# Turning the softmax maxima on VectorE, squares on GpSimd, and a new order of the starts, in a two-block transformer kernel

## The chip, the cores and the metric

The kernel runs as one program on one core of one Trainium2 chip (trn2). The metric is the device time of one execution in microseconds. A core has five engines with queues of their own: TensorE (PE), VectorE (DVE), ScalarE (ACT), GpSimd (POOL) and SyncE (SP), which here only issues DMAs. They wait for each other on semaphores.

## The reference

Two transformer blocks on x [B=8, T=512, C=256], float32. Each block is modulated by a vector made from c, with layer norm ahead of each half:

```python
h = _layernorm(x) * (1 + ca) + sa
x = x + ga * _L0_attn_ref(h, ...)      # rms-normed q and k, rope, 16 heads of 16, softmax(q k / 4 + 1)
h = _layernorm(x) * (1 + cb) + sb
x = x + gb * _L0_ffn_ref(h, ...)       # ternary weights, 1024 wide
# the second block the same way:
x = x + ga * _L1_attn_ref(h, ...)      # biases, no rms norm, no rope; output divided by its mean norm
x = x + gb * _L1_ffn_ref(h, ...)       # layer norm, 8 experts of 1024, gelu, next_w
```

The change touches the two attention halves only. In layer 0 they are

```python
q = (x @ wq.T).reshape(B, T, H, hd); k = ...; v = ...
q, k = rms(q), rms(k)                  # var = mean(t * t, axis=-1) + EPS over the 16 of a head
q, k = rope(q), rope(k)
scores = einsum('bhtd,bhsd->bhts', q, k) * scale + 1.0
y = einsum('bhts,bhsd->bhtd', softmax(scores), v) @ wproj.T
```

## The kernel before

The program runs four parts one after the other: attention of layer 0 (to about 583 us), the feed-forward net of layer 0 (to about 1282 us), attention of layer 1 (1282 to about 1812 us) and the experts (to the end). The change lies in `attention(nc, layer, d, keep)`, which builds the first and third.

Precision: float32 products are made of fp16 high and low halves. Queries and keys stand in SBUF as `QS` and `KT`, 128 partitions x 8 head pairs x 512 tokens, in two blocks of partitions (a = 0 and 1, one head of each pair). A block holds three runs of 16 rows, high and low halves, so that one matmul over 48 rows gives the score. A 49th row of `QS` (index QROWS - 1) carries the negated maximum of each query, and a matmul over 49 rows gives the score less its maximum.

Order of the work: a table gives every step of a batch its slot. `PAIRS` = 32 slots are one batch, 8 slots are one group G of four heads, and each engine runs `for p in range(BEGIN, END)` through the same slots in order. `AT0` and `AT1` hold the slots of the steady state, relative to their batch; `EARLY0` and `EARLY1` those of the first batches, from slot -140 on, ahead of slot 0 of batch 0. In slot p TensorE does: raw scores 2p+AHEAD (L1028, into one of two banks `SM`), the two final scores of pair p (L1045, into `ST`), raw scores 2p+AHEAD+1, then the slot's job, and the products with the values (L1064, into `AV`). `raw` waits until VectorE has read the bank two raws before.

- The maximum. VectorE reduces each 128x512 block of raw scores (L824) to one column of `M`, negated, fp16. In slot 8G-5 the job `MT` has TensorE turn `M` by four transposes (L964) into the PSUM bank `X`; ScalarE copies it to `MTs` (L596, 4 x 512) a slot later; and SyncE copies it a slot after that by two DMAs (L356) of two partitions each into the 49th rows. The first scores of the group (slot 8G) wait for these. `M` and `MTs` are doubled.
- The bank `X`. It is shared by all jobs outside the start: T0, T1 (turning the normed tokens, L969), QK0 to QK3 and V0, V1 (projections, L934), H0 to H3 (turning q and k, L1000), YT, P and MT. They go through it in the order of `jobs`, and each waits until the one before was copied out (`out`).
- Layer 0 norm and rope. After each QKi ScalarE reads the bank twice: Copy to `qraw` (L613) and Square to `sq` (L616). VectorE sums the squares by head (L886, step SUM), GpSimd adds epsilon (VAR, L533), ScalarE makes the first guess of the root (RMSG, L706 and L708), GpSimd does a Newton step (INV, L455 to L461) and the rotation (ROT, L488 to L502, about 5.1 us a tile), ScalarE the high half (HI, L718), GpSimd the low half (LOW, L510).
- To the heads' layout. The H jobs turn q and k, VectorE copies them out (L841), SyncE stores four tiles of 256 KB a batch to DRAM (`store_features`, L332, tensor `qk`) and loads them as 12 DMAs of 128 KB (HIGH and LOWS, L343 and L349), 16 partitions each. In layer 1 ScalarE and GpSimd make the halves from the projections directly.
- Weights for the next part. In layer 0, 32 parts of the feed-forward weights are loaded, split by GpSimd (L449, L451), checked by VectorE with one maximum each (L891) and stored, at the slots of `STAGE_AT`: four a batch.
- Modulation. Three groups of small matmuls, at the slots of `MOD_AT`.
- The tokens of batch n+1 are loaded (L361, `xt`) after XN of batch n has read those of batch n; STAT (L868) reads them.

The scores of a group's first slot wait for its two row copies:

```python
if u == 0 and a == 1:
    pe.wait_ge(row_ld[G % 2], 32 * (G // 2 + 1))
```

Of the kernel before, what the change touches and what calls it, by code (L numbers as in the profile page):

```python
# [109 lines left out]
AHEAD = 28  # L110


def placed(base, table):
# [27 lines left out]
OWN_BANK = {("T0", 0): "X", ("T1", 0): "AV", ("V0", 0): "SM0", ("V1", 0): "SM1"} | {(f"QK{i}", 0): f"ST{i}" for i in range(4)}
OWN_BANK0 = OWN_BANK | {(f"QK{i}", 1): f"ST{i}" for i in range(4)} | {(f"H{i}", 0): ("X", "AV", "SM0", "SM1")[i] for i in range(4)}
STAGE_AT = [PAIRS * (i // 4) + (20, 22, 25, 27)[i % 4] for i in range(4 * B)]


def attention(nc, layer, d, keep):
# [28 lines left out]
    with ExitStack() as ctx:  # L175
# [393 lines left out]
        def _(act):  # L569
# [73 lines left out]
            for p in range(BEGIN, END):  # L643
# [1442 lines left out]
```

## Time and profile before

| | |
|---|---|
| time, 3 runs | 2191.36, 2195.03, 2197.32 us; median 2195.03 us |
| profiled execution | 2191.5 us, its span 2189.8 us |
| TensorE matmuls | 1880.9 us busy (86%), x10573 |
| weight loads | 767.0 us (35%) |
| VectorE | 1350.6 us (62%), x2591 |
| ScalarE | 1211.6 us (55%), x1686 |
| GpSimd | 576.3 us (26%), x668 |
| DMA | 147.90 MB, mean 68 GB/s, q1 25.3% of 16 engines |

The span runs from the first to the last instruction of the profiled execution; the execution's own time is 1.7 us longer. The busy shares are means over four parts with different limits, so the two attention parts are read by windows of time. The batches of layer 0 lie at 109.5 to 172.5, 172.5 to 235.4, 235.4 to 296.9, 296.9 to 358.2, 358.2 to 419.2, 419.2 to 481.7, 481.7 to 536.8 and 536.8 to 583.2 us. Those of layer 1 begin at 1357.0, 1416.0 and 1478.3 us; the last ends at 1812.3 us. The times ahead of 109.5, and from 1282.0 to 1357.0, are the starts of the two layers.

### The profile page before, as it was taken

To read this page: it belongs to the slowest core of one execution; us is meant where nothing else is said; L and a number is where in the kernel's file an instruction comes from. 1 tells how busy PE (TensorE), PEld (TensorE's weight loads), DVE (VectorE), ACT (ScalarE), POOL (GpSimd) and SP (SyncE) were. 2 spreads that over 40 slices of the span, in tenths; PEclk is the share of its full clock that TensorE was granted. 3 is DMA by queue.
4 is the path that set the end of the run, shared out by engine and by line. 5 is a ranking of instruction groups with operands and counts; after the bars stand their busy time and mean duration, and the time that the engine had idled before them with its cause. 6 is when DMAs were issued, how large, how long until landed. Compare 5 with 4: busy or idle time off the path is not lost. (4 is left out here: it accounts for less than half of the span.)

```text
span 2189.8 us, 29709 instructions
## 1 busy us (share of the span) xinstructions
PE 1880.9 (86%) x10573; PEld 767.0 (35%) x10573; DVE 1350.6 (62%) x2591; ACT 1211.6 (55%) x1686; POOL 576.3 (26%) x668
## 2 busy tenths in 40 slices
PE   5789999988759999999999956898889983888897
PEld 3323333222224444444444421232223221444443
DVE  5578888878433553553554424777777873677672
ACT  4377888767623432432432233787778873565563
POOL 4676766642200000000000041111111001343443
PEclk8689999999969999999999975999999996899999
DMA  2343554433260000000000023333333304323210
GB/s 107 69 112 88 122 131 108 121 109 85 73 232 1 20 21 12 10 20 11 10 20 1 10 67 53 59 59 59 69 68 59 59 11 160 116 92 129 89 39 19
DMA packets 111985, 147.90 MB, mean 68 GB/s; under 512 B 11874, under 2 KB 95188, under 8 KB 109780
## 3 DMA queue, kind: packets, MB, share of 16 engines
q1 hardware_dynamic: 111828, 145.77, 25.3%
q8 instruction: 103, 1.69, 0.3%
q14 instruction: 54, 0.44, 0.1%
HBM read 100.34 MB, written 45.14 MB: 66 GB/s over the span
## 5 line engine op out<-in xcount | busy, mean ns | idle before, releaser
L824 DVE TENSOR_REDUCE A_M<-A_SM 128x1 f16<-128x512 f32 x1024 | 652.8, 685 | 179.2 <-PE A_SM L1028 177.1
L587 ACT ACTIVATE A_P<-A_ST 128x1024 f32<-128x1024 f32 x512 | 524.0, 1026 | 152.8 <-PE A_ST L1045 148.2
L1028 PE MATMUL A_SM<-A_KT,A_QS 48*128 48x512 f16 x1024 | 358.3, 404 | 78.4 <-DVE A_M L824 67.8
L1337 PE MATMUL B_PA<-B_Hh,B_wh 128*128 128x512 f16 x1024 | 388.1, 379 | 0.0
L1337 PE MATMUL B_PA<-B_Hl,B_wh 128*128 128x512 f16 x1024 | 388.1, 379 | 0.0
L1241 ACT ACTIVATE B_af<-B_PA,B_sv 128x512 f32<-128x512 f32 x192 | 132.0, 688 | 358.1 <-PE B_PA L1337 358.0
L1045 PE MATMUL A_ST<-A_QS,A_KT 49*128 49x512 f16 x1024 | 304.9, 391 | 0.1
L1064 PE MATMUL A_AV<-A_P,A_V 128*32 128x512 f32 x2048 | 280.0, 610 | 5.6 <-ACT A_P L587 5.0
L1028 PEld LDWEIGHTS A_SM<-A_KT,A_QS 48*128 48x128 f16 x1024 | 81.7, 94 | 461.0 <-DVE A_M L824 403.6
L1302 DVE TENSOR_SCALAR B_Hh<-B_af 128x512 f16<-128x512 f32 x128 | 57.9, 452 | 269.7 <-ACT B_af L1241 269.7
L1197 POOL TENSOR_TENSOR B_hl<-B_hf,B_hh 128x512 f16<-128x512 f32 x16 | 18.5, 1157 | 547.8 <-ACT B_hh L1224 547.8
L1337 PEld LDWEIGHTS B_PA<-B_Hl,B_wh 128*128 128x128 f16 x1024 | 100.2, 98 | 119.3
L1337 PEld LDWEIGHTS B_PA<-B_Hh,B_wh 128*128 128x128 f16 x1024 | 100.2, 98 | 119.2
L1304 DVE SCALAR_TENSOR_TENSOR B_Hl<-B_af,B_Hh 128x512 f16<-128x512 f32 x128 | 88.7, 693 | 4.4
L559 POOL TENSOR_TENSOR A_tr<-A_qkf,A_tr 128x512 f16<-128x512 f32 x32 | 37.0, 1159 | 196.5 <-ACT A_tr L681 196.4
L1296 DVE SCALAR_TENSOR_TENSOR B_uf<-B_PD,B_sv,B_af 128x512 f32<-128x512 f32 x64 | 47.8, 747 | 48.4 <-PE B_PD L1337 24.3
L520 POOL TENSOR_TENSOR A_hl<-A_hf,A_hh 128x512 f16<-128x512 f32 x32 | 36.8, 1158 | 121.0 <-ACT A_hh L665 121.0
L1064 PEld LDWEIGHTS A_AV<-A_P,A_V 128*32 128x32 f32 x2048 | 44.6, 108 | 63.7 <-issue 50.3
L868 DVE BATCH_NORM_STATS2 A_st<-A_xt 128x6 f32<-128x256 f32 x64 | 25.1, 416 | 65.6 <-DMA A_xt<-x_tok 60.0
L1337 PE MATMUL B_PA<-B_hh,B_wh 128*128 128x512 f16 x128 | 51.1, 399 | 14.3 <-issue 14.3
L1045 PEld LDWEIGHTS A_ST<-A_QS,A_KT 49*128 49x128 f16 x1024 | 55.8, 94 | 15.3 <-ACT A_P L587 12.6
L969 PE MATMUL A_X<-id,A_xn 128*128 128x128 f32 x120 | 22.8, 321 | 44.5 <-ACT A_xn L688 29.0
(308 smaller groups left out, 3335.8 us busy)
## 6 DMA issues: line engine op xcount, KB each, us to landing
D_w_st<-in_we_dram SPq DMA_DIRECT2D x16, 1024.0 KB, 4.9
qk<-A_tr SPq DMA_DIRECT2D x62, 256.0 KB, 2.4
A_KT<-qk SPq DMA_DIRECT2D x96, 128.0 KB, 4.7
A_QS<-qk SPq DMA_DIRECT2D x96, 128.0 KB, 5.2
A_w_st<-in_w_ffn_dram SPq DMA_DIRECT2D x32, 352.0 KB, 3.8
w_hi<-A_f_hi SPq DMA_DIRECT2D x32, 176.0 KB, 3.5
w_lo<-A_f_lo SPq DMA_DIRECT2D x32, 176.0 KB, 3.6
B_wl<-w_lo SPq DMA_DIRECT2D x1, 5632.0 KB, 25.1
```

The costliest lines, as they stand in the source:

```text
L520: nc.gpsimd.tensor_tensor(hl[:, f, :], hf[:, f, :], hh[:, f, :], ALU.subtract).then_inc(h_low, 1)
L559: nc.gpsimd.tensor_tensor(tr[2 * (i // 2) + 1][:, i % 2, :], qkf[:, i % 2, :], tr[2 * (i // 2)][:, i % 2, :], ALU.subtract).then_inc(qk_lo ...
L587: nc.scalar.activation(P[:, st, 2 * pair:2 * pair + 2, :], ST[:, u % 2, :, :], ACT.Exp, scale=1.0 / math.sqrt(HD)).then_inc(exp_s, 1)
L824: nc.vector.tensor_reduce(M[G % 2][:, tt, o:o + 1], SM[:, n % 2, :], AX, ALU.max, negate=True).then_inc(max_s, 1)
L1028: nc.tensor.matmul(SM[:, n % 2, :], QS[b % 2][r, 2 * g + pair, tt * 128:tt * 128 + 128], KT[b % 2][r, 2 * g + pair, :], start=True, stop=T ...
L1045: ins = nc.tensor.matmul(ST[:, u % 2, a, :], KT[b % 2][r, pair, o:o + 128], QS[b % 2][r, pair, :], start=True, stop=True)
L1064: ins = nc.tensor.matmul(AV[32 * j:32 * j + 32, :], V[b % 3][:, st, g * HG + j, :], P[:, st, j, :], start=st == 0, stop=st == TT - 1)
L1241: nc.scalar.activation(af[:, s % 3, :], PA[:, s % 4, :], ACT.Silu if s < HM else ACT.Gelu, scale=sv[:, which, m:m + 1]).then_inc(a_out, 1)
L1296: nc.vector.scalar_tensor_tensor(out=uf[:, s % 2, :], in0=PD[:, s % 2, :], scalar=sv[:, 1, s:s + 1], in1=src, op0=ALU.mult, op1=ALU.mult). ...
L1302: nc.vector.tensor_scalar(Hh[w][:, m, :], src, HS, None, ALU.mult).then_inc(high, 1)
L1304: nc.vector.scalar_tensor_tensor(out=Hl[w][:, m, :], in0=src, scalar=HS, in1=Hh[w][:, m, :], op0=ALU.mult, op1=ALU.subtract).then_inc(spli ...
L1337: ins = nc.tensor.matmul(out, a, c, start=start and kt == 0 and n_ == 0, stop=stop and kt == kts[-1] and n_ == len(ops) - 1)
```

## The change

1. The job MT is gone. VectorE writes the maxima into `M` [128, 32] and, in slot 8G-5 after its first maximum, transposes the 32x32 blocks of `M` into `rows`. SyncE copies these a slot later (8G-4) with eight DMAs of 8 partitions x 64 bytes each. `X16` and `MTs` are gone. GpSimd clears `M` once.
2. `AHEAD` is 26 for 28.
3. In layer 0, from batch 2, ScalarE reads a QK bank once (Copy) and GpSimd squares `qraw` into `sq`, in the slots SQ. SUM, VAR, RMSG, INV, ROT, HI and LOW come one to three slots later.
4. Both starts have new tables. In layer 0: earlier transposes and projections of batch 1, HI and LOW of batch 0 between them, H jobs two slots earlier, tokens of later batches normed at other slots, the third part of the modulation earlier. In layer 1: all QK projections of batch 1 ahead of the loads, in banks of their own, and GpSimd's clearing of the second buffers after batch 1's low halves.
5. The weight parts: two a batch in batches 0 to 4, and 22 every third slot from 185 to 248.
6. The DRAM tensor `qk` is laid out by head block, so that a load reads 8 KB in one run per partition, and a store writes with the head index within four as its outermost dimension.

```diff
 PAIRS = 32
-AHEAD = 28
+AHEAD = 26
...
 AT0 = placed(-80, dict(STAT=(-51, -48, -45, -43), AGG=-41, ROOT=-40, XN=(-27, -26, -24, -22), T0=-1, T1=1, HH=(0, 2), HL=(1, 3),
-                       QK0=10, QK1=12, QK2=18, QK3=20, V0=26, V1=28, SUM=(12, 14, 20, 22), VAR=(15, 24), RMSG=(16, 26),
-                       INV=(17, 27), ROT=(17, 21, 27, 31), HI=(22, 27, 35, 37), LOW=(24, 28, 36, 38),
+                       QK0=10, QK1=12, QK2=18, QK3=20, V0=26, V1=28, SQ=(11, 13, 20, 22), SUM=(14, 15, 23, 24), VAR=(16, 26), RMSG=(17, 27),
+                       INV=(18, 28), ROT=(18, 22, 29, 32), HI=(23, 28, 36, 38), LOW=(25, 29, 37, 39),
...
                             QK0=10, QK1=11, QK2=12, QK3=13, V0=14, V1=15, SUM=(12, 13, 15, 15), VAR=(13, 15), RMSG=(13, 15),
-                            INV=(14, 17), ROT=(16, 16, 17, 17), HI=(17, 18, 19, 20), LOW=(18, 19, 20, 21),
-                            H0=30, H1=31, H2=32, H3=33, HIGH=(36, 36, 36, 36, 37, 37, 37, 37), LOWS=(38, 38, 38, 38))),
-          placed(-140, dict(STAT=(10, 10, 10, 10), AGG=11, ROOT=11, XN=(16, 16, 16, 16), T0=21, T1=23, HH=(22, 24), HL=(23, 25),
-                            QK0=25, QK1=26, QK2=27, QK3=28, V0=40, V1=42, SUM=(29, 29, 34, 35), VAR=(30, 34), RMSG=(31, 35),
-                            INV=(32, 37), ROT=(33, 36, 48, 50), HI=(37, 39, 128, 133), LOW=(38, 40, 129, 134),
+                            INV=(14, 17), ROT=(16, 16, 17, 17), HI=(17, 19, 22, 24), LOW=(18, 20, 23, 25),
+                            H0=28, H1=29, H2=30, H3=31, HIGH=(34, 34, 34, 34, 34, 34, 34, 34), LOWS=(35, 35, 35, 35))),
+          placed(-140, dict(STAT=(10, 10, 10, 10), AGG=11, ROOT=11, XN=(16, 16, 16, 16), T0=18, T1=20, HH=(19, 21), HL=(20, 22),
+                            QK0=23, QK1=24, QK2=25, QK3=26, V0=32, V1=33, SUM=(27, 27, 33, 33), VAR=(28, 34), RMSG=(29, 40),
+                            INV=(30, 42), ROT=(31, 41, 44, 45), HI=(39, 42, 129, 133), LOW=(40, 43, 130, 134),
                             H0=137, H1=139, H2=140, H3=141, HIGH=(143, 143, 144, 144, 145, 145, 146, 146), LOWS=(147, 147, 148, 148))),
-          placed(-140, dict(STAT=(35, 35, 36, 36), AGG=37, ROOT=37, XN=(41, 41, 41, 41), T0=44, T1=46, HH=(45, 47), HL=(46, 47))),
-          placed(-140, dict(STAT=(127, 128, 130, 131), AGG=132, ROOT=133, XN=(135, 136, 138, 139))),
-          dict(STAT=(4, 5, 6, 6))]
+          placed(-140, dict(STAT=(18, 18, 18, 18), AGG=19, ROOT=26, XN=(31, 31, 31, 31), T0=35, T1=37, HH=(36, 38), HL=(37, 39))),
+          placed(-140, dict(STAT=(128, 129, 130, 131), AGG=132, ROOT=135, XN=(143, 144, 146, 147))),
+          dict(STAT=(10, 11, 12, 13), AGG=(14,), ROOT=(15,))]
 EARLY1 = [placed(-140, dict(STAT=(0, 0, 0, 0), AGG=1, ROOT=2, XN=(3, 3, 3, 3), T0=4, T1=5, HH=(5, 6), HL=(6, 7),
-                            QK0=10, QK1=11, QK2=12, QK3=13, V0=14, V1=15, HIGH=(18, 18, 18, 18, 19, 19, 19, 19), LOWS=(20, 20, 20, 20)))]
-MOD_AT = (-138, -134, -106)
+                            QK0=10, QK1=11, QK2=12, QK3=13, V0=14, V1=15, HIGH=(18, 18, 18, 18, 18, 18, 18, 18), LOWS=(19, 19, 19, 19))),
+          placed(-140, dict(STAT=(12, 12, 12, 12), AGG=13, ROOT=13, XN=(21, 21, 21, 21), T0=23, T1=25, HH=(24, 26), HL=(25, 27),
+                            QK0=28, QK1=29, QK2=30, QK3=31, HIGH=(36, 36, 36, 36, 36, 36, 36, 36), LOWS=(38, 38, 38, 38))),
+          placed(-140, dict(STAT=(132, 133, 135, 136), AGG=137, ROOT=138, XN=(142, 144, 146, 150))),
+          dict(STAT=(13, 14, 16, 17), AGG=(18,), ROOT=(19,))]
+MOD_AT = (-138, -134, -120)
+MOD_PE = (-138, -134, -118)
 OWN_BANK = {("T0", 0): "X", ("T1", 0): "AV", ("V0", 0): "SM0", ("V1", 0): "SM1"} | {(f"QK{i}", 0): f"ST{i}" for i in range(4)}
-OWN_BANK0 = OWN_BANK | {(f"QK{i}", 1): f"ST{i}" for i in range(4)} | {(f"H{i}", 0): ("X", "AV", "SM0", "SM1")[i] for i in range(4)}
-STAGE_AT = [PAIRS * (i // 4) + (20, 22, 25, 27)[i % 4] for i in range(4 * B)]
+OWN_BANK |= {(f"QK{i}", 1): f"ST{i}" for i in range(4)}
+OWN_BANK0 = OWN_BANK | {(f"H{i}", 0): ("X", "AV", "SM0", "SM1")[i] for i in range(4)}
+STAGE_AT = [PAIRS * b + o for b in range(B - 3) for o in (21, 25)] + [PAIRS * B - 71 + 3 * i for i in range(22)]
...
         QS = [sb(f"QS{k}", [128, H // 2, T], F16) for k in range(2)]
-        M = [sb(f"M{k}", [128, TT, HG], F16) for k in range(2)]
-        MTs = [sb(f"MT{k}", [HG, T], F16) for k in range(2)]
+        M, rows = ([sb(f"{n}{k}", [128, 32], F16) for k in range(2)] for n in ("M", "rows"))
...
-            return d["qk"][n % 2, which, :, :].rearrange("(p a d) t -> a d p t", a=2, d=HD)[a]
+            return d["qk"][n % 2, which, a, :, :, :]
...
                     sp.wait_ge(qk_ld[n % 2], 192 * (n // 2))
-                sp.dma_start(d["qk"][n % 2, which, :, :].rearrange("(f p) t -> p f t", p=128), tile[:, :, :]
+                sp.dma_start(d["qk"][n % 2, which, :, :, :, :].rearrange("a d (f q) t -> q (a d) f t", f=FT), tile[:, :, :]
...
             for p in range(BEGIN, END):
-                G = group_at(p, -3)
+                G = group_at(p, -4)
                 if G is not None:
-                    sp.wait_ge(*out("MT", G))
+                    sp.wait_ge(row_s, G + 1)
+                    g, k = G % NG, (G // NG) % 2
                     for a in range(2):
-                        sp.dma_start(QS[(G // NG) % 2][BLK * a + QROWS - 1:BLK * a + QROWS, 2 * (G % NG):2 * (G % NG) + 2, :],
-                                     MTs[G % 2][2 * a:2 * a + 2, :]).then_inc(row_ld[G % 2], 16)
+                        row = QS[k][BLK * a + QROWS - 1:BLK * a + QROWS, 2 * g:2 * g + 2, :].rearrange("o p (t x) -> o (p t) x", t=TT)
+                        for i in range(4):
+                            sp.dma_start(row[:, :, 32 * i:32 * i + 32], rows[G % 2][32 * i + 8 * a:32 * i + 8 * a + 8, :]
+                                         ).then_inc(row_ld[G % 2], 16)
...
                 un = qraw[:, tt, :]
-                pool.wait_ge(q_raw, r + 1)
+                if n == 1:
+                    pool.wait_ge(q_raw, r + 1)
...
                         nc.gpsimd.tensor_tensor(hl[:, f, :], hf[:, f, :], hh[:, f, :], ALU.subtract).then_inc(h_low, 1)
-                if p == slots_of("HL", 0)[1] + 1:
+                if p == slots_of(*(("HL", 0) if L0 else ("HL", 1)))[1] + 1:
                 if L0:
+                    for tt in range(TT):
+                        n = at(p, "SQ", tt)
+                        if n is not None and n >= 2:
+                            pool.wait_ge(*out(f"QK{tt}", n))
+                            pool.wait_ge(q_sum, TT * n + tt - 1)
+                            nc.gpsimd.tensor_tensor(sq[:, tt % 2, :], qraw[:, tt, :], qraw[:, tt, :], ALU.mult).then_inc(q_sq, 1)
...
-                if name == "MT":
-                    act.wait_ge(*done(name, n))
-                    if n >= 2:
-                        act.wait_ge(row_ld[n % 2], 32 * (n // 2))
-                    nc.scalar.activation(MTs[n % 2][:, :], X16[0:HG, 0:T], ACT.Copy).then_inc(out(name, n)[0], 1)
-                elif name in ("T0", "T1"):
+                if name in ("T0", "T1"):
...
                         act.wait_ge(q_rot, 4 * rotations(n - 1, tt) + 4)
-                    nc.scalar.activation(qraw[:, tt, :], bank(name, n), ACT.Copy, scale=1 / WS).then_inc(q_raw, 1)
+                    nc.scalar.activation(qraw[:, tt, :], bank(name, n), ACT.Copy, scale=1 / WS
+                                         ).then_inc(q_raw if n < 2 else job_out, 1)
+                    if n >= 2:
+                        return
...
                 if t == 0 and G >= 2:
-                    dve.wait_ge(*done("MT", G - 2))
+                    dve.wait_ge(row_s, G - 1)
+                if t == 0 and G < 2:
+                    dve.wait_ge(m_init, G + 1)
                 dve.wait_ge(raw_mm, n + 1)
-                o = 2 * a + pair
-                nc.vector.tensor_reduce(M[G % 2][:, tt, o:o + 1], SM[:, n % 2, :], AX, ALU.max, negate=True).then_inc(max_s, 1)
+                o = 8 * a + TT * pair + tt
+                nc.vector.tensor_reduce(M[G % 2][:, o:o + 1], SM[:, n % 2, :], AX, ALU.max, negate=True).then_inc(max_s, 1)
+
+            def turn_maxima(G):
+
+                dve.wait_ge(max_s, 16 * (G + 1))
+                if G >= 2:
+                    dve.wait_ge(row_ld[G % 2], 128 * (G // 2))
+                nc.vector.transpose(rows[G % 2][:, :], M[G % 2][:, :]).then_inc(row_s, 1)
...
                         if n is not None:
-                            dve.wait_ge(*out(f"QK{tt}", n))
+                            if n < 2:
+                                dve.wait_ge(*out(f"QK{tt}", n))
+                            else:
+                                dve.wait_ge(q_sq, TT * (n - 2) + tt + 1)
...
                 maximum(2 * p + AHEAD)
+                G = group_at(p, -5)
+                if G is not None:
+                    turn_maxima(G)
...
                     pe.wait_ge(ones_s, 1)
-                if name == "MT":
-                    pe.wait_ge(max_s, 16 * (n + 1))
-                    for tt in range(TT):
-                        ins = nc.tensor.transpose(X16[0:HG, tt * 128:tt * 128 + 128], M[n % 2][:, tt, :], id16[:, :])
-                elif name in ("T0", "T1"):
+                if name in ("T0", "T1"):
...
                     pe.wait_ge(*out("V1", 0))
-                    if L0:
-                        pe.wait_ge(*out("QK3", 1))
+                    pe.wait_ge(*out("QK3", 1))
                 if u == 0 and a == 1:
-                    pe.wait_ge(row_ld[G % 2], 32 * (G // 2 + 1))
+                    pe.wait_ge(row_ld[G % 2], 128 * (G // 2 + 1))
...
         x2_tok, modrow = dram("x2_tok", [B, T, C]), dram("modrow", [B, 12, 128])
-        qk = dram("qk", [2, 4, C, T], F16)
+        qk = dram("qk", [2, 4, 2, HD, H // 2, T], F16)
```

## Rows read from the trace of the kernel before

**Rows 1.** windows, six stretches; columns: stretch, length, PE, PEld, DVE, ACT, POOL, clock, DMA, GB/s

```profile
0.00:109.50 109.50, 67.70 (x308) 38.97 (x308) 56.95 (x135) 40.99 (x74) 61.05 (x91) 0.73 0.32 88
...
296.90:358.20 61.30, 56.16 (x399) 18.98 (x399) 52.58 (x95) 49.61 (x71) 43.28 (x54) 1.00 0.45 109
...
481.70:536.80 55.10, 46.32 (x318) 12.88 (x318) 47.65 (x81) 38.36 (x45) 11.44 (x10) 1.00 0.45 111
...
536.80:583.20 46.40, 40.26 (x276) 11.08 (x275) 29.93 (x51) 36.76 (x43) 11.41 (x10) 1.00 0.20 67
...
1282.00:1357.00 75.00, 36.78 (x119) 12.91 (x120) 24.82 (x57) 25.48 (x40) 31.78 (x42) 0.59 0.36 75
...
1416.00:1478.30 62.30, 54.43 (x358) 17.32 (x357) 45.69 (x86) 47.60 (x65) 9.45 (x14) 0.95 0.31 60
```

**Rows 2.** waits, all engines: engine and line <- releaser: total us, times, longest

```profile
PEld A_SM L1028 <- DVE A_M L824: 403.6, 593, 5.1
```

**Rows 3.** grouped lines of both attention layers: busy us, mean ns | idle before, releaser

```profile
L824 DVE TENSOR_REDUCE A_M<-A_SM 128x1 f16<-128x512 f32 x1024 | 652.8, 685 | 179.2 <-PE A_SM L1028 177.1
...
L964 PE MATMUL A_X<-id,A_M 128*4 128x128 f16 x256 | 25.6, 225 | 22.3 <-DVE A_xT L832 11.5 <-ACT A_sq L616 5.4 <-ACT A_qkf L624 2.4
...
L596 ACT ACTIVATE A_MT<-A_X 4x512 f16<-4x512 f16 x64 | 36.6, 572 | 4.5 <-PE A_X L964 4.5
...
L616 ACT ACTIVATE A_sq<-A_X 128x512 f32<-128x512 f32 x24 | 14.2, 592 | 0.0
...
L488 POOL TENSOR_TENSOR A_qraw<-A_qraw,A_rr 128x512 f32<-128x512 f32 x28 | 29.7, 1059 | 1.1
...
L891 DVE TENSOR_REDUCE A_f_max<-A_f_lo 128x1 f32<-128x704 f16 x32 | 27.9, 875 | 3.1 <-POOL A_f_lo L451 3.1
```

**Rows 4.** timeline of TensorE: start us, duration, line, count, idle before and releaser

```profile
331.66 0.60 PE L1045 MATMUL A_ST<-A_QS,A_KT 49*128 49x512 f16 x2
...
334.08 0.33 PE L964 MATMUL A_X<-id,A_M 128*4 128x128 f16 x3 [1.82 <-DVE A_xT L832]
...
335.26 0.60 PE L1045 MATMUL A_ST<-A_QS,A_KT 49*128 49x512 f16 x2
...
554.51 0.60 PE L1045 MATMUL A_ST<-A_QS,A_KT 49*128 49x512 f16 x2
...
555.42 0.33 PE L964 MATMUL A_X<-id,A_M 128*4 128x128 f16 x3
...
556.60 0.60 PE L1045 MATMUL A_ST<-A_QS,A_KT 49*128 49x512 f16 x2
...
562.49 0.50 PE L1045 MATMUL A_ST<-A_QS,A_KT 49*128 49x512 f16 x2
```

**Rows 5.** timeline of SyncE's queue, two copies of rows

```profile
305.12 1.20 SPq L356 DMA_DIRECT2D A_QS<-A_MT  x2
```

**Rows 6.** DMA issues: count, KB each, us to landing; the smallest copy

```profile
A_b<-A_bl SPq DMA_DIRECT2D x1, 0.5 KB, 1.6
```

**Rows 7.** timeline, starts of both layers and the wait for tokens

```profile
83.21 1.29 DVE L824 TENSOR_REDUCE A_M<-A_SM 128x1 f16<-128x512 f32 x2 [13.80 <-PE A_SM L1028]
...
1300.32 3.51 POOL L426 MEMSET A_KT<- 128x4096 f16 x1
...
1311.58 0.34 SPq L343 DMA_DIRECT2D A_KT<-qk  x1
...
1328.39 1.41 DVE L868 BATCH_NORM_STATS2 A_st<-A_xt 128x6 f32<-128x256 f32 x4 [27.98 <-DMA A_xt<-x_tok]
...
1420.91 0.43 DVE L868 BATCH_NORM_STATS2 A_st<-A_xt 128x6 f32<-128x256 f32 x1 [4.21 <-DMA A_xt<-x_tok]
```

**Rows 8.** DMA issues: stores of qk, a store of x, loads of tokens

```profile
qk<-A_tr SPq DMA_DIRECT2D x62, 256.0 KB, 2.4
...
x<-A_xT SPq DMA_DIRECT2D x8, 512.0 KB, 3.1
...
A_xt<-x_tok SPq DMA_DIRECT2D x8, 512.0 KB, 3.8
```

More of the change, by code:

```diff
@@ L159, in attention @@
     jobs = {slots_of(name, n)[0]: (name, n) for name in names for n in range(B)}
-    jobs |= {8 * G - 5: ("MT", G) for G in range(B * NG)}
-    assert len(jobs) == B * len(names) + B * NG
+    assert len(jobs) == B * len(names)
     shared = [job for p, job in sorted(jobs.items()) if job not in own]
@@ L223, in attention @@
         AV, X = pb("AV", [128, T]), pb("X", [128, T])
-        X16 = X[:, :].bitcast(F16)
         w_ld, w_high, w_split, wp_ld, tab_ld, tab = (sem(n) for n in ("w_ld", "w_high", "w_split", "wp_ld", "tab_ld", "tab"))
@@ L240, in attention @@
         job_done, job_out = sem("job_done"), sem("job_out")
+        q_sq = sem("q_sq")
+        m_init, row_s = sem("m_init"), sem("row")
         early_done, early_out, turned_done, turned_out = (sem(n) for n in ("early_done", "early_out", "turned_done", "turned_out"))
@@ L438, in _ @@
                 nc.gpsimd.memset(ones2[:, :], 1.0).then_inc(ones_s, 1)
+            for k in range(2):
+                nc.gpsimd.memset(M[k][:, :], 0.0).then_inc(m_init, 1)
             pool.wait_ge(const, 2 if L0 else 1)
@@ L645, in _ @@
                 if name[:2] == "QK" or name[0:1] == "V":
-                    out_of_bank(name, n)
-                name, n = jobs.get(p - 1, ("", 0))
-                if name == "MT":
                     out_of_bank(name, n)
@@ L947, in job @@
                     pe.wait_ge(*out(("T1", "T1", "V0", "V1")[int(name[1])], 0))
+                    if name == "H1":
+                        pe.wait_ge(mod_moved, 3)
                     if name == "H0":
@@ L960, in job @@
                     pe.wait_ge(ones_s, 1)
-                if name == "MT":
-                    pe.wait_ge(max_s, 16 * (n + 1))
-                    for tt in range(TT):
-                        ins = nc.tensor.transpose(X16[0:HG, tt * 128:tt * 128 + 128], M[n % 2][:, tt, :], id16[:, :])
-                elif name in ("T0", "T1"):
+                if name in ("T0", "T1"):
                     f = int(name[1])
@@ L1059, in values @@
                     elif L0:
-                        pe.wait_ge(mod_moved, 3)
+                        pe.wait_ge(*out("H1", 0))
                     else:
@@ L1072, in modulation @@
                 if i == 2:
-                    pe.wait_ge(*out("H1", 0))
+                    pe.wait_ge(*out("T1", 0))
                 for m in range(m0, m1):
@@ L1083, in _ @@
             for p in range(BEGIN, END):
-                if L0 and p in MOD_AT:
-                    modulation(MOD_AT.index(p))
+                if L0 and p in MOD_PE:
+                    modulation(MOD_PE.index(p))
                 raw(2 * p + AHEAD)
```

## The prediction

> **What bounds the kernel now.** I read the windows by batch first [rows 1]: one line a stretch, with each engine's busy time and the clock granted. Both attention layers run one written order of slots, 32 a batch, 8 a group of four heads, and no engine fills a whole window: in 296.9 to 358.2 TensorE is busy 56.2 of 61.3 us, VectorE 52.6, ScalarE 49.6, GpSimd 43.3. So a slot costs what its longest chain costs. Then the waits [rows 2]: the raw scores' weight load waits 403.6 us for VectorE's maximum over 593 times; the maxima themselves [rows 3] are 1024 of 685 ns and pace the thin slots. The grouped lines [rows 3] also give what the change takes out: 256 TensorE transposes of 225 ns with 22.3 us of idle time before the matmuls, and 64 ScalarE copies of 572 ns. Last, the timeline of TensorE [rows 4]: in the slot from 331.66 to 335.26 (3.60 us) the transposes of the maxima stand 1.82 us behind a VectorE copy out of the shared bank X; in the quiet stretch the slot with them, 554.51 to 556.60, takes 2.09 us. The time goes where the bank X, TensorE's order and VectorE's maxima meet, in slots 3, 11, 19 and 27 of each batch.
>
> **The MT job goes.** Per group: 4 transposes, one ScalarE copy (0.57, beside other ScalarE work, which has 11 us to spare in the window of 61) and the hand-over of X. The floor is the transposes alone: 4 x 0.22 = 0.9 us, less where VectorE's maximum is what the slot waits for. In the quiet slot the neighbours without jobs take about 1.5, so 0.5 to 0.6 is freed; in the slot of 3.60 the wait of 1.82 goes too, but VectorE's copy, two maxima and the transpose block remain in order, so 1.5 of it. Slots 3, 11, 19, 27 of a layer-0 batch: 0.9 + 0.5 + 1.5 + 0.9 = 3.8. Layer 1 has no projection job there: 4 x 0.6 = 2.4, taken as 2.5. It costs VectorE one transpose of 32x32 blocks per group. No row shows one; bounds: 0.18 (below any full-width row) to 0.69 (a maximum [rows 3]); it has 32 columns, so I take 0.2, and it waits for the last of 16 maxima, which its own engine has just done, and for row copies of two groups before, long landed; behind it stand the second maximum of the slot, and the raw scores that wait for that.
>
> **The row DMAs.** SyncE issues eight copies a group instead of two, a slot earlier. Two take 1.20 [rows 5], so eight take 4.8. In the quiet group slot 554.51 is the slot of the transposes and scores that need the row start at 562.49: 7.98, and 7.4 once the transposes are out. The chain: first maximum 0.9 into the slot (the transposes start at 555.42), block transpose up to 0.7, seven issues 4.2, landing 1.6 [rows 6]: 7.4. The slack shrinks to between 0 and 0.8. I price it at nothing in most groups, since slots with jobs are longer; if the slack is gone, each 0.1 of lateness costs 6.4 us over the 64 groups. The same 4.8 stands ahead of the qk stores and of the loads of tokens on SyncE's queue.
>
> **Layer 0, squares on GpSimd.** From batch 2, 24 tiles leave ScalarE's Square (592 ns) for GpSimd: nearest row its product of the same shape, 1059 ns [rows 3]; I take 1.1. GpSimd then holds 43.3 + 4 x 1.1 = 47.7 of 61, less two of four weight parts that move on. Cover: VectorE's sums are placed one to three slots later and the root, Newton steps and rotations one slot later. If cover is gone, VectorE's in-order queue, and with it the maxima, waits: up to 2 us at slot 10 of a batch. Copies come out of X 0.6 earlier. I take +0.8 a batch. Net for batches 1 to 5: 3.8 - 0.8 = -3.0, five times, -15. Batch 0: its first slots run at what the prologue left; -2.
>
> **Stage parts.** 22 parts move to slots 185 to 248. Each puts an 875 ns maximum on VectorE [rows 3], which is busy 47.7 of 55.1 in batch 6 [rows 1]. Batches 0 to 4 keep 2 of 4; batch 5 holds 3, batch 6 ten, batch 7 nine: 11 more in the last two, 11 x 0.87 = 9.6 us of VectorE work; bounds 0 and +9.6. Batch 6 has 7.4 us of VectorE free, batch 7 has 46.4 - 29.9 = 16.5 [rows 1], but their thin slots wait for maxima already [rows 4]; I take half, +5, less 8 groups x 0.4 for the MT job: +2.
>
> **Prologues.** Layer 0: from the first maximum, 83.21 [rows 7], to the end of the first window, 109.50, where the first slot begins, lie 26.3 us. AHEAD 26 for 28 drops two of 28 maxima (1.29 for two): -1.3. 28 maxima are 18.1 of the 26.3; 8.2 are jobs between them (QK, V, casts and rotations of batch 1), of which half is now done during the 13.80 us in which VectorE waits for the loads: -4. The H transposes, two slots earlier and behind fewer jobs: -2.7 (bounds 0, -6). Sum -8. Layer 1: a memset of 3.51 and two small ones ahead of the first low halves [rows 7] move behind batch 1's: some 2 of it are on the path to the stores (bounds 0 and 3.5); two raws -1.3; QK of batch 1 in its own banks ahead of the loads instead of between the maxima of the window of 75.0 us: -5.7 (bounds 0, -9). Sum -9, and -3 for batch 0 of layer 1, whose tokens now are read ahead of time.
>
> **The wait for tokens in layer 1.** VectorE waits 4.21 us for the next batch's tokens at 1420.91 [rows 7], in a batch that spends 62.3. The load they wait for now stands behind eight row copies on SyncE's queue instead of two, 6 x 0.6 = 3.6 us more in the worst case, 0 where the queue is idle before it; the value nearest to an idle queue, +1, for 5 batches: +5. For batch 1 the wait of 27.98 at 1328.39 goes: it is inside the -9.
>
> **Stores and loads of qk.** The store writes q outermost, runs of 1 KB as before; the loads read 8 KB runs. A store lands in 2.4, and twice the bytes in 3.1 [rows 8], so 0.7 is its transfer. The loads of a layer's start, from the first issue at 1311.58 to 1328.39 [rows 7], take 16.8 us for 2 MB (12 loads and one of tokens), 125 GB/s. I take both as unchanged; bounds: rivals 1 and 2. The Trainium skill, "SBUF — State Buffer", section "Door 1: The DMA port swizzle", says that a transfer's rate depends on how many SBUF ports its partitions reach, which for 16 neighbouring partitions are few. By that, longer runs give nothing; the 125 GB/s of these loads, which reach 16 partitions each, agrees.
>
> **Sum**, against the profiled execution's own 2191.5: -8 - 2 - 15 + 2 - 9 - 3 + 5 and batches 1 to 6 of layer 1, 6 x -2.5 = -15: -45, so 2146.5. The median of the runs shown, 2195.03, lies 3.5 above the profiled one: **2150**.
>
> **Rivals.**
> 1. *The stores run narrow.* Their outermost dimension on the DRAM side is now 4 where it was 128. If only 4 of 16 engines carried each, the 0.7 of transfer is 2.8, landing 4.5 for 2.4, and stores in a row queue on the same four: the first loads +4 in each prologue, the tokens' load of five layer-1 batches behind two stores +2 each: +18, so 2168. For it: the rule of the Trainium skill, "DMA: Bandwidth & Descriptors", section "Why a DMA increments its semaphore by 16 and not by 1", that the number of engines is the largest up to 16 that divides the slowest dimension of both sides. No run here shows a 4. Against: the old row shows only 128-wide stores. Chance 0.25.
> 2. *Long runs help.* If 8 KB runs loaded like the tokens, prologue loads of 15 us shrank by a third to two thirds: -6 each, 2138. Against: tokens in 1 KB runs load faster already [rows 8], so the run isn't the limit. Chance 0.08.
> 3. *Slower: the rows land late everywhere.* SyncE at 0.75 us an issue (a 2-partition copy takes 0.6) makes the chain 1.0 longer than 7.4; scores of each of 64 groups then wait. The point where the gain of 45 is eaten is 0.7 us a group. At 0.9 an issue plus a queue of stores, 1.2 us a group: 2150 + 75 = 2225. For it: seven issues in a row, slack 0 to 0.8. Against: the copies read 8 partitions of 64 bytes and write one, no bigger than before. Chance 0.11.
> 4. *GpSimd late.* The squares stand behind rotations of 5.1 us a tile; VectorE's sum then holds the maxima 3 us a batch, six batches: 2168 less what stages gave, 2164. Chance 0.14.
>
> **How the numbers follow.** Forecast 0.42, rivals as given. A measurement here tells 0.3%, 6.6 us, from no change: 2188.4 to 2201.6. Rivals 1, 2, 4 and the forecast stay below; some of them add (1 with 4 is 2182), and 0.07 is left within. Faster 0.82, same 0.07, slower 0.11. Range 2118 to 2185: the sum's bounds on prologues and stages (-30, +30 about) and the faster rivals; rival 3 is left out.
>
> **What would show it.** In the profile after: no transposes nor copies of MT; slot of the projection 3.6 down to 2.1; 512 row copies of 0.6; no wait of the scores' weight load on them, else rival 3. First scores of layer 0 at about 101 and layer 1's prologue 66 for 75. Store landings 2.4 or 4.5 (rival 1); loads of a batch in 15 or 10 us (rival 2); VectorE's idle before the sums on GpSimd (rival 4). Wrong altogether if the windows of batches 1 to 5 aren't some 3 shorter.

## The result, and the profile after

The changed kernel takes 2292.93 us (median of 4 runs, 2290.8 to 2294.79) against 2193.2 us before: ratio 1.0456, 95% interval 1.043 to 1.0482. It is slower by 100 us where a gain of 45 was forecast. The profiled execution took 2292.0 us, its span is 2290.3.

The windows of the changed kernel (columns as in [rows 1]): the start of layer 0, its batches 0, 3 and 6, the start of layer 1, and layer 1's batch 1.

```profile
0.00:107.90 107.90, 68.58 (x304) 41.90 (x305) 57.27 (x134) 37.30 (x67) 63.67 (x95) 0.72 0.33 87
107.90:184.00 76.10, 57.81 (x358) 18.48 (x357) 51.95 (x97) 45.98 (x61) 40.39 (x52) 0.84 0.35 84
304.60:363.40 58.80, 54.88 (x380) 18.50 (x380) 51.47 (x97) 46.10 (x63) 42.68 (x54) 1.00 0.37 88
479.60:546.40 66.80, 55.20 (x299) 12.50 (x299) 51.85 (x89) 35.85 (x40) 27.34 (x24) 0.82 0.60 168
1299.50:1382.40 82.90, 38.83 (x119) 13.21 (x119) 24.30 (x57) 24.43 (x38) 32.99 (x45) 0.60 0.49 99
1438.50:1513.70 75.20, 55.91 (x340) 17.53 (x340) 46.24 (x90) 46.60 (x62) 9.43 (x14) 0.84 0.25 50
```

Batch 3 of layer 0 is what the change was forecast to do: 58.8 for 61.3 [rows 1]. Batch 1 of layer 1 takes 75.2 for 62.3, with VectorE and ScalarE busy for about as long as before, so most of the 13 us is waiting; the granted clock fell from 0.95 to 0.84 with it. The waits of the whole kernel name the places (engine and line <- releaser: total, times, longest):

```profile
PEld A_ST L1069 <- DMA A_QS<-A_rows: 61.1, 24, 7.8
DVE A_st L889 <- DMA A_xt<-x_tok: 56.7, 7, 10.7
```

In the first, some 60 us, the first scores of a group wait for their rows; the list of before has no such line. The second is the wait of [rows 7]. Its sum was 60.0 before, but 28.0 of that was the one wait at the start of layer 1; inside batches 1 to 4 it was 2.6 to 4.2 us each, and now it is 9.3 to 9.8. The timelines of a stretch of layer 1, SyncE's queue, VectorE, TensorE, show both:

```profile
1432.29 5.39 SPq L364 DMA_DIRECT2D A_QS<-A_rows  x8
1437.79 1.25 SPq L337 DMA_DIRECT2D qk<-A_tr  x2
1439.09 1.97 SPq L369 DMA_DIRECT2D A_xt<-x_tok  x1
...
1449.10 0.43 DVE L889 BATCH_NORM_STATS2 A_st<-A_xt 128x6 f32<-128x256 f32 x1 [9.37 <-DMA A_xt<-x_tok]
...
1463.13 1.25 SPq L337 DMA_DIRECT2D qk<-A_tr  x2
1469.94 0.34 SPq L348 DMA_DIRECT2D A_KT<-qk  x1
...
1474.97 5.48 SPq L364 DMA_DIRECT2D A_QS<-A_rows  x8
...
1485.67 0.61 PE L1069 MATMUL A_ST<-A_QS,A_KT 49*128 49x512 f16 x2 [7.22 <-DMA A_QS<-A_rows]
```

*The tokens.* Their load is issued 1.3 us behind the first of two stores of qk and lands 10.0 us later (3.8 in [rows 8]). A DMA's semaphore counts to sixteen. In the trace's semaphore records the first of these stores has one record at 1.0 us and then four, at 5.6, 5.8, 6.7 and 6.8 us; the second ends at 9.2. Before, a store had sixteen records within 0.2 us, at 2.0 to 2.2. The load behind them has twelve of its sixteen by 5.3 us and the last four at 8.6 to 10.0. So four engines carry the stores, and the load waits for its share on those four. That is rival 1, and the records agree with the rule of the Trainium skill that the rival named ("DMA: Bandwidth & Descriptors", "Why a DMA increments its semaphore by 16 and not by 1").

*The rows.* SyncE takes its work in order. It waits for the first store of a pair to land (1463.13 + 6.8) before it issues the first load of qk at 1469.94; ten loads and a store of `y` stand ahead of the row copies, which are issued 2.9 us after VectorE's transpose ended. They land 5.8 us after the last issue, behind these loads. In the kernel with the old layout (e1, below) the same wait is 1.86 us: the loads are issued 2.2 us after the stores, the row copies at once, and they land in 3.4. These two delays, 2.9 and 2.4 us, make up the difference between 7.22 and 1.86.

Where the 100 us lie, from the first exponential of each batch in the two traces:

| stretch | before | after | forecast | measured |
|---|---|---|---|---|
| start of layer 0 | 110.6 | 108.9 | -8 | -1.6 |
| its batch 0 | 62.6 | 76.1 | -2 | +13.5 |
| batches 1 to 5 | 309.0 | 295.6 | -15 | -13.4 |
| batches 6, 7, to the last exponential | 101.4 | 120.5 | +2 | +19.1 |
| from there to layer 1's first exponential | 774.4 | 781.9 | -9 | +7.5 |
| layer 1, to its last exponential | 454.8 | 529.6 | -13 | +74.8 |

The forecast prices the start of layer 1 alone in its fifth row; the stretch also holds the feed-forward net.

### The profile page after: what moved, and what is told of

Same layout as the page of the kernel before. It is cut to its first block and busy times, and to the rows that moved or that the text cites. A ratio compares the mean times of both kernels' runs of the same rounds, so it can differ in the third digit from the quotient of the medians.

```text
span 2290.3 us, 29544 instructions
## 1 busy us (share of the span) xinstructions
PE 1899.2 (83%) x10317; PEld 763.7 (33%) x10317; DVE 1362.6 (59%) x2655; ACT 1176.5 (51%) x1598; POOL 600.7 (26%) x696
## 5 line engine op out<-in xcount | busy, mean ns | idle before, releaser
L838 DVE TENSOR_REDUCE A_M<-A_SM 128x1 f16<-128x512 f32 x1024 | 659.6, 684 | 255.6 <-PE A_SM L1053 251.5
L1053 PE MATMUL A_SM<-A_KT,A_QS 48*128 48x512 f16 x1024 | 375.5, 416 | 132.1 <-DVE A_M L838 102.6
L1069 PE MATMUL A_ST<-A_QS,A_KT 49*128 49x512 f16 x1024 | 313.6, 407 | 60.8 <-DMA A_QS<-A_rows 60.4
L1088 PE MATMUL A_AV<-A_P,A_V 128*32 128x512 f32 x2048 | 290.8, 642 | 6.7 <-ACT A_P L604 6.3
L1069 PEld LDWEIGHTS A_ST<-A_QS,A_KT 49*128 49x128 f16 x1024 | 55.5, 95 | 84.2 <-DMA A_QS<-A_rows 61.1
L1361 PE MATMUL B_PA<-B_hh,B_wh 128*128 128x512 f16 x128 | 50.7, 396 | 19.2 <-issue 19.1
```

The costliest lines, as they stand in the source:

```text
L838: nc.vector.tensor_reduce(M[G % 2][:, o:o + 1], SM[:, n % 2, :], AX, ALU.max, negate=True).then_inc(max_s, 1)
L1053: nc.tensor.matmul(SM[:, n % 2, :], QS[b % 2][r, 2 * g + pair, tt * 128:tt * 128 + 128], KT[b % 2][r, 2 * g + pair, :], start=True, stop=T ...
L1069: ins = nc.tensor.matmul(ST[:, u % 2, a, :], KT[b % 2][r, pair, o:o + 128], QS[b % 2][r, pair, :], start=True, stop=True)
L1088: ins = nc.tensor.matmul(AV[32 * j:32 * j + 32, :], V[b % 3][:, st, g * HG + j, :], P[:, st, j, :], start=st == 0, stop=st == TT - 1)
L1361: ins = nc.tensor.matmul(out, a, c, start=start and kt == 0 and n_ == 0, stop=stop and kt == kts[-1] and n_ == len(ops) - 1)
```

## The experiments

"Old layout" is part 6 undone; "MT back" is part 1 undone. Each ratio is to the kernel before, run beside it on the same chip. The experiments ran on several chips; the kernel before had medians of 2191.3 to 2192.9 us there.

**The layout, four runs.** Part 6 undone in the changed kernel (e1), done alone in the kernel before (e2), undone together with part 1 (e3), and a third layout that keeps the store 128 wide (e4):

```diff
 # e1, e3: old layout (e2 has these lines the other way round, in the kernel before)
-qk = dram("qk", [2, 4, 2, HD, H // 2, T], F16)
+qk = dram("qk", [2, 4, C, T], F16)
-sp.dma_start(d["qk"][n % 2, which, :, :, :, :].rearrange("a d (f q) t -> q (a d) f t", f=FT), tile[:, :, :])
+sp.dma_start(d["qk"][n % 2, which, :, :].rearrange("(f p) t -> p f t", p=128), tile[:, :, :])
 ...   # and the loads' view to match
 # e4
+qk = dram("qk", [2, 4, 128, FT, T], F16)
+sp.dma_start(d["qk"][n % 2, which, :, :, :], tile[:, :, :])
+heads: d["qk"][n % 2, which, :, :, :].rearrange("(q a d) f t -> a d f q t", a=2, d=HD)[a]
 # e3 also: the MT job, its ScalarE copy and its two row copies a group, as before
```

> The changed kernel with part 6 alone undone: qk laid out in DRAM as before, the store's outermost dimension 128 again, the loads in 1 KB runs. Theory N (narrow stores): a store of 256 KB was carried by 4 of 16 DMA engines and took some 9 us for a pair, and the tokens' load, the qk loads and the row copies stood behind it on those four engines. Then nearly all of the loss goes: layer-1 slot 0 falls from 11.2 to about 5 us, slot 15 from 8.8 to below 3, the kernel comes to 2160 to 2200 us. Rival R (eight row copies of 0.64 us on SyncE are late by themselves): slot 15 stays at 8 or so and the kernel stays above 2240 us. Rival S (the new tables of the starts and slots): no change, 2280 to 2295 us.

> The kernel before with part 6 alone done: the new DRAM layout of qk, store and loads, nothing else. Theory N: slower by 40 to 80 us against before (2235 to 2275), stores land in 6 to 9 us, layer-1 slot 0 near 11 us. Rival R or S: within 10 us of before, 2190 to 2203.

> The changed kernel with part 6 undone and part 1 undone as well: the maxima turned on TensorE and copied by ScalarE, two row copies a group. Theory N with a working turn on VectorE: this one is slower than the one with part 6 alone undone, by 20 to 30 us, the price forecast for the MT job (3.8 and 2.4 us a batch). Rival R: it is faster than that one, by 10 us or more, since two copies a group land in time and eight don't.

> The changed kernel with a third layout of qk in DRAM, tile partition outermost: a store writes 2 KB runs with an outermost dimension of 128, the loads read 2 KB runs. Theory N: as fast as with the old layout, 2160 to 2200 us, within 5 us of it, stores landing in 2.0 to 2.5 us; if longer runs help at all, a few us faster. If narrow stores are not the cause but the long runs of the loads or the order of the starts is, it stays at 2280 to 2295.

| | median us | ratio, 95% interval |
|---|---|---|
| e1 | 2210.7 | 1.0079 [1.0055, 1.0103] |
| e2 | 2283.2 | 1.0413 [1.038, 1.0447] |
| e3 | 2186.4 | 0.9983 [0.9965, 1.0001] |
| e4 | 2213.3 | 1.0088 [1.0056, 1.0119] |

The layout costs 82 us in the changed kernel and 92 in the one before. e4 has the store 128 wide and reads runs of 2 KB, and takes as long as e1. Long runs alone behind a wide store (8 KB) were not run, so between them and the width of the store the traces decide: the loads of KT land in a median of 5.0 us with 8 KB runs, 4.7 with 2 KB and 4.8 with 1 KB, while the stores go from 2.2 to 6.8 and 9.2. The width of the store is the cause. Here are the stores' landing in e1 and e4 (the profile gives none for e2), then what waits in e2, whose rows come from the two copies of MT:

```profile
qk<-A_tr SPq DMA_DIRECT2D x62, 256.0 KB, 2.5
```
```profile
qk<-A_tr SPq DMA_DIRECT2D x62, 256.0 KB, 2.3
```
```profile
DVE A_st L868 <- DMA A_xt<-x_tok: 81.8, 8, 34.0
PEld A_ST L1045 <- DMA A_QS<-A_MT: 34.1, 14, 4.1
```

Even two row copies are late behind narrow stores. But e1 is still slower than before, at a time that neither theory N nor rival R had, and e3 is faster than e1 by 24: the eight row copies are a second loss, as rival R said. In e1 their waits are 26.1 us, for 61.1 in the changed kernel, and the issues are 0.635 us each. The window is that of layer 1's batch 1 in e1:

```profile
L364 SPq DMA_DIRECT2D A_QS<-A_rows x512: 634/635/1464, 93.0 to 1820.7; - x171
...
  PEld A_ST L1069: 26.1, 11
```
```profile
1407.50:1472.30 64.80, 57.70 (x340) 17.63 (x340) 46.16 (x90) 46.54 (x61) 9.45 (x14) 0.87 0.30 58
```

**The row copies.** e5 has four of them, each from 16 partitions to the two rows; in e6 and e7 ScalarE and GpSimd issue these four in layer 1:

```diff
-for a in range(2): row = QS[k][BLK * a + QROWS - 1:BLK * a + QROWS, ...]
-    for i in range(4): sp.dma_start(row[...], rows[G % 2][32 * i + 8 * a:32 * i + 8 * a + 8, :])
+row = QS[k][QROWS - 1:BLK + QROWS:BLK, ...]
+for i in range(4): sp.dma_start(row[...], rows[G % 2][32 * i:32 * i + 16, :])
```

> The changed kernel with the old layout of qk, and four row copies a group instead of eight (16 partitions to two rows each). Theory I (the number of issues): each costs 0.64 us on SyncE, the chain is 2.5 us shorter, layer-1 slot 15 falls from 4.6 to about 2 us and the thin slots 0 mod 8 of the last batch by 0.3; 2190 to 2198 us against the 2210.7 of eight copies. Theory Q (queue): in layer 1 the row packets wait behind twelve loads of 128 KB on the same DMA engines, so the landing of the third group stays late, slot 15 stays at 3.5 to 4.6 us; 2203 to 2212.

> As the kernel with four row copies, but in layer 1 ScalarE issues them from its own queue. Theory Q: they no longer stand behind SyncE's loads, landings of the third group fall from about 4.5 to 1.7 us after the last issue, slot 15 to 1.3 us; but the four issues cost ScalarE up to 2.6 us a group, 32 groups in layer 1, so the time may come out even. Theory I: the landing is as late as with SyncE issuing four.

> As the kernel with four row copies, but in layer 1 GpSimd issues them, which has 50 us a batch to spare there. Theory Q: slot 15 of layer 1 about 1.3 us if the queue of GpSimd lands in under 3 us; 2185 to 2195 in all. If GpSimd's issues cost over 1 us each, the rows come later in every group and layer 1 grows by 1 to 2 us a group: 2220 to 2260. Theory I: no better than with SyncE issuing four.

Measured: e5 2164.3 (0.987 [0.9849, 0.989]), e6 2174.3 (0.9918 [0.9891, 0.9944]), e7 2161.3 (0.9869 [0.9845, 0.9893]). Four copies are worth 46 us, far more than theory I said (13 to 21), and they make the changed kernel faster than the one before. In e5 an issue takes 0.496 us, and the weight loads wait 1.4 us in all for rows (26.1 in e1). What made the other 20 us was not separated. The batch of layer 1 shown above:

```profile
L363 SPq DMA_DIRECT2D A_QS<-A_rows x256: 495/496/687, 93.2 to 1777.5; - x128
```
```profile
1396.90:1456.10 59.20, 53.84 (x340) 16.99 (x340) 46.20 (x90) 45.92 (x62) 9.45 (x14) 0.94 0.34 63
```

ScalarE as the issuer costs 10 us; GpSimd is as good as SyncE within the noise. Theory Q had a gain for both, theory I none: with four copies little waiting for rows is left to save.

e5 against e3 is also the price of the MT job, both with wide stores and rows in time: 22 us in the medians. In the traces batches 1 to 5 of layer 0 are 17.6 us shorter without it, 3.5 a batch. But the feed-forward net, whose code is the same in all, takes 653.6 to 654.0 us from its first matmul to its end in the five kernels with the MT job (before, e2, e3, e8, e10) and 658.0 to 663.5 in the fourteen without it. Its window and that of the start of layer 1, before and in e14 (below):

```profile
624.40:1278.00 653.60, 637.25 (x2992) 298.61 (x2992) 301.53 (x606) 215.94 (x300) 16.20 (x14) 0.99 0.06 20
1285.90:1358.00 72.10, 37.78 (x122) 13.13 (x122) 25.28 (x57) 24.20 (x40) 28.01 (x40) 0.59 0.36 71
```
```profile
594.60:1253.90 659.30, 637.87 (x2992) 297.59 (x2992) 302.51 (x606) 216.69 (x300) 16.20 (x14) 0.98 0.06 20
1261.80:1324.20 62.40, 38.98 (x123) 13.77 (x125) 24.36 (x57) 22.66 (x37) 29.20 (x41) 0.64 0.64 109
```

In e5 TensorE stands idle for 1.2 to 1.5 us ahead of five matmuls of the net that have a gap of at most 0.1 in e3, and the profile names nothing that it waited for. Why is open.

**Eight copies, a slot more.** e13 keeps eight, with AHEAD 28 and the turn in slot 8G-6; e16 does so in layer 1 alone.

```diff
-AHEAD = 26
+AHEAD = 28
-    G = group_at(p, -4)     # SyncE
+    G = group_at(p, -5)
-    G = group_at(p, -5)     # VectorE
+    G = group_at(p, -6)
```

> Old layout, eight row copies, but AHEAD 28 again and both the turn on VectorE and the copies one slot earlier. Theory I (the chain of eight issues of 0.64 us and the landing has no slack): a slot of 1.3 to 1.8 us is more than what is missing in nearly all groups, so most of the 46 us that eight copies cost against four comes back: 2168 to 2182 in place of 2210.7. Rival (their number loads the queue or delays SyncE's other work, whatever the slack): 2195 to 2215.

> Old layout, eight row copies, the turn and the copies one slot earlier with AHEAD 28 in layer 1 alone, layer 0 as in the kernel with eight copies (2210.7). Theory I (the chain of eight has no slack; in layer 0 the earlier slot met SyncE's token loads): layer 1 shorter by 20 to 25 us, 2186 to 2192. Rival: the gain of layer 1 in the last run was chance of where layer 0 ended, 2205 to 2213.

e13: 2211.1 (1.0079 [1.0059, 1.0098]), no change from e1, so theory I missed. The trace said why: of the 26.1 us of waiting for rows 3.7 are left, layer 1 is 24 us shorter (459.2 for 482.8 from first to last exponential), and layer 0 is 18 us longer (494.7 for 476.5), where a new wait stands. The timeline of SyncE's queue and VectorE in e13, and its wait for the tokens of layer 0 (13.4 us in e1):

```profile
228.20 5.41 SPq L364 DMA_DIRECT2D A_QS<-A_rows  x8
233.65 0.44 SPq L369 DMA_DIRECT2D A_xt<-in_x_tok_dram  x1
...
238.05 0.43 DVE L889 BATCH_NORM_STATS2 A_st<-A_xt 128x6 f32<-128x256 f32 x1 [5.99 <-DMA A_xt<-in_x_tok_dram]
```
```profile
DVE A_st L889 <- DMA A_xt<-in_x_tok_dram: 29.5, 5, 6.6
```

The eight issues now stand in front of the tokens' load. e16 moved layer 1's part alone: 2191.1 (0.9985 [0.9969, 1.0001]), 20 us faster than e1, as theory I had it. So eight copies cost in two ways that are one: 5.4 us of SyncE's queue, which makes late either the rows or what is behind them. The rest of the way to e5, 27 us, was not traced.

**Weight parts.** e8 is e3 with `STAGE_AT` as before; e15 is e14 (below) with the same.

> Old layout, maxima turned on TensorE again, and STAGE_AT as before (four weight parts a batch): left of the change are AHEAD, the new starts and the squares on GpSimd. Theory: the 22 parts in the last batches cost 9 us in batch 6 and 1 in batch 7, and what they free in batches 0 to 5 is about 5; with them undone the time is 2178 to 2184 against 2186.4. Rival: the parts moved free more in the job-heavy batches than they cost, and it gets slower, 2188 to 2195.

> The same with the weight parts at four a batch as before. With the maxima turned on TensorE this made no difference (2187.2 to 2186.4). The same expected here, within 4 us of the one before; if VectorE's extra 875 ns each are what bounds batches 6 and 7 once MT is gone, 4 to 8 us faster.

e8: 2187.2, e3: 2186.4. e15: 2146.7, e14: 2145.4. No difference either way in the sum, but in the traces two differences cancel: with the parts moved, batches 1 to 5 are 7.2 us shorter (308.5 in e3, 315.7 in e8) and batches 6 and 7 are 8.0 us longer. Between e15 and e14 it is 5.8 and 6.0.

**The squares and the tokens' slots.** e9 is e5 with ScalarE squaring (AT0's slots as before); e10 is the kernel before with part 3 alone; e11 is e5 with these lines as before; e12 is e7 with them; e14 is e9 with them; e17 is e14 with GpSimd issuing layer 1's rows.

```diff
-placed(-140, dict(STAT=(128, 129, 130, 131), AGG=132, ROOT=135, XN=(143, 144, 146, 147))),
-dict(STAT=(10, 11, 12, 13), AGG=(14,), ROOT=(15,))
+placed(-140, dict(STAT=(127, 128, 130, 131), AGG=132, ROOT=133, XN=(135, 136, 138, 139))),
+dict(STAT=(4, 5, 6, 6))
```

> The kernel with the old layout and four row copies, and part 3 undone: ScalarE squares from PSUM again in every batch, with the slots of the sums, roots, rotations and halves as before. What the squares on GpSimd are worth by themselves: theory G, forecast in the prediction as a cost of up to 2 us a batch that is hidden: the time is 2161 to 2168, as with the squares on GpSimd (2164.3). Rival: ScalarE and the bank X are relieved and it gets slower by 6 to 15 us without it; or GpSimd's squares stall VectorE's sums and it gets faster by 5 to 12.

> The kernel before with part 3 alone done: from batch 2 GpSimd squares, with the later slots. Theory G: within 4 us of before, 2187 to 2195. If the squares stall the sums: 2198 to 2205. If X is relieved while the maxima still go through it: 2180 to 2186.

> The kernel with the old layout and four row copies, and the slots at which the tokens of batches 3 and 4 are normed as before, so that the load of batch 4's tokens is issued ahead of batch 1's qk loads again. Theory: the 6.4 us for which VectorE waits for it in slot 10 of batch 0, and the half clock after it, go: 2153 to 2159. Rival: the norming of batch 3 ahead of slot 0 makes the start of layer 0 longer by as much: 2161 to 2167.

> The best combination: old layout, four row copies, in layer 1 issued by GpSimd, and the old slots of those tokens. If the two gains add, 2150 to 2156; if row copies from GpSimd are worth nothing, as the version with SyncE's.

> Old layout, four row copies, squares on ScalarE, and the tokens of batches 3 and 4 normed in the slots of before. If the two gains (13 and 7 us against 2164.3) add: 2142 to 2147. If both came from the same stalls of layer 0's first batches: 2149 to 2153, as with the squares alone moved back.

> Old layout, four copies, squares on ScalarE, tokens as before, and in layer 1 the rows issued by GpSimd. With SyncE issuing them it is 2145.4. GpSimd's queue was worth 0 to 3 us before; 2140 to 2147 here.

| | median us | ratio, 95% interval |
|---|---|---|
| e9 | 2151.0 | 0.9804 [0.9781, 0.9826] |
| e10 | 2199.6 | 1.0032 [1.002, 1.0044] |
| e11 | 2157.2 | 0.9827 [0.9805, 0.9849] |
| e12 | 2156.7 | 0.9846 [0.9822, 0.987] |
| e14 | 2145.4 | 0.9789 [0.9773, 0.9805] |
| e17 | 2150.7 | 0.9804 [0.9784, 0.9824] |

The squares on GpSimd cost 7 us alone (e10, interval 4 to 10) and 13 in e5 (e9). The window of batch 3 of layer 0 in e5, the waits about the squares in it, and the same window in e9:

```profile
289.00:347.90 58.90, 55.16 (x382) 18.52 (x380) 51.59 (x97) 46.19 (x63) 42.72 (x55) 1.00 0.39 88
```
```profile
POOL A_sq L540 <- ACT A_qraw L624: 5.0, 2, 2.6
...
ACT A_rln L717 <- POOL A_rv L549: 1.9, 1, 1.9
```
```profile
277.70:334.60 56.90, 55.09 (x386) 18.62 (x384) 51.19 (x97) 47.54 (x67) 38.74 (x50) 1.00 0.41 91
```

GpSimd takes its work in order: it waits for ScalarE's copy ahead of a square (5.0 us), its variance step (L549) comes after, and ScalarE waits 1.9 us for that with the exponentials behind it. The batch is 2.0 us longer for 1.4 us of ScalarE work saved. The profile shows no wait for the squares themselves. The tokens' slots gave 7 us in e11, 4.7 in e12 and 5.6 in e14. Each is near the noise of one comparison, all three have the same sign, and batch 0 of layer 0 is 3.1, 4.7 and 1.3 us shorter in the traces. e14 is the best version, 2.1% below the kernel before; e17 is not better (2140 to 2147 was expected).

## Why the prediction was wrong

The step that failed first is "I take both as unchanged" under **Stores and loads of qk**: the store was priced as before, though its outermost dimension went from 128 to 4. That cost 82 us (e1) to 92 (e2). Rival 1 had the mechanism and named the place, but its +18 was mis-sized. It took a landing of 4.5 us; the first store of a pair took 6.8 and the second 9.2. It gave the tokens' load +2 a batch; VectorE waits 6.3 us longer than in e1 (9.37 for 3.04). And it had no term for SyncE's own order: the loads of qk are not issued until a store has landed, and the row copies stand behind them, 5.4 us more a batch (7.22 for 1.86). The two are 11.7 us of waiting in a batch that is 10.4 longer than in e1. The granted clock fell as well (0.84 for 0.87); no run separates what it costs by itself.

The second is **The row DMAs**: "I price it at nothing in most groups". The chain was sized well: eight issues of 0.635 us for 0.6, landing 1.6 to 1.7 in most groups, a slack of at most 0.8 in 48 of e1's 64 groups. But in 14 groups no slack is left, and four copies gave 46 us back (e5). Rival 3 said that this could eat the gain, but by issues of 0.75 us and in every group. What happened is narrower. In the third group of each layer-1 batch the row packets land behind the loads of qk, 3.4 to 5.0 us after the last issue, and SyncE's 5.4 us delay what is behind them (e13). The landing of 1.6 was read from another DMA [rows 6]. The semaphore records of the kernel before have 3.4 to 5.1 us for the row copies of just these groups, in batches 1 to 6, and 1.6 in the other groups of these batches, so this could have been read ahead of time.

Third, **Layer 0, squares on GpSimd**: taken as +0.8 a batch, they cost 2.0 in batch 3 and 13 us in all. Rival 4 had 14, but that is luck: its mechanism, VectorE's sum waiting for the squares, shows nowhere; ScalarE waits for GpSimd's variance step (6.8 us in e5, 1.1 in e9), and the rest was not traced. Fourth, **Prologues**: batch 0 was put at -2, but moving the norming of batch 3 put the load of batch 4's tokens behind the qk loads; 5 to 7 us (e11, e12, e14). I had not priced this move at all. Fifth, **Stage parts** took +5 in the last two batches and left out what the parts free in batches 1 to 5: 6 to 8 and -6 to -7 were measured. Sixth, no term stood for the feed-forward net, 4.4 us longer in the changed kernel and 5.7 in e14.

What held: the MT job in layer 0, 3.5 us a batch for 3.8; the start of layer 0 once the stores are wide, where the first slot begins at 101.0 us in e1 for 109.5, -8.5 for -8; the start of layer 1, from its first token statistics to its first exponential, 72.1 us before, 63.2 in e1 and 62.4 in e14, -9 and -10 for -9; the transpose on VectorE, 0.20 us; the square, 1.04 us for 1.1. Loads with 8 KB or 2 KB runs were no faster than with 1 KB (medians 5.0 and 4.7 for 4.7), so rival 2 shows nowhere.

Some agreement is luck. Batches 1 to 5 of layer 0 came out at -13.4 for -15, but the parts are -17.6 for the MT job, +6.0 for the squares, -7.2 for the weight parts and +4.6 for the narrow stores, read from pairs of traces. Layer 1 in e14 takes 441.1 us from first to last exponential, -13.7 for -13. In that, the +5 for the tokens didn't come (their waits are 2.6 to 2.9 us), and batch 0 has +0.7 for -3. And five kernels with the same layer 1 (e5, e9, e11, e14, e15) have 439.4 to 450.7, so one trace doesn't settle a difference of 10 us there. The change as it was forecast, with wide stores and four row copies, is e5: -27 us for -45. e14's 2145.4, near the sum's 2150, has the squares and the tokens undone as well.

## What to carry to other kernels

Look at the outermost dimension of both sides of a DMA before its run lengths: made 4 for longer reads, it put a store on four engines and delayed everything that came behind it in the queue, not only the store. Count the DMAs that a step issues, not its bytes: the issuing queue is an in-order engine, and a step moved onto it, or ahead on it, moves all that stands behind. Take a DMA's landing time from the place in the queue where it will stand: the same two row copies landed in 1.6 us by themselves and in up to 5.1 behind the loads of qk. A step moved to an engine with spare busy time costs where its results are waited for in order.

## What the runs showed of the hardware

- Of a pair of 256 KB stores with an outermost dimension of 4 the first landed 6.8 us after its issue and the second 9.2, and held back a 512 KB load to 10.0; with 128 outermost the stores of e1's layer-1 batches took 2.16 to 2.65 us.
- The issue of a 0.5 KB row copy of 8 partitions took 0.635 us on SyncE, of 1 KB and 16 partitions to two rows 0.496; the latter took 0.51 on ScalarE's queue and 0.557 on GpSimd.
- In the kernel before, the second of two row copies landed 3.4 to 5.1 us after its issue behind the loads of 128 KB, in the third group of layer-1 batches 1 to 6, and 1.6 us after it in their other groups.
- VectorE's transpose of 32x32 blocks in a 128x32 fp16 tile took 0.20 us.
- Of layer-1 batches with the same work, those of 75 us with TensorE waiting in them were granted a clock of 0.84, those of 58.1 us (e14) 0.97.
